# Splitting the layer-normalised activations in fp16 where they lie and transposing them by DMA instead of on TensorE

## The reference, cut to what matters

```python
h = relu(hypergraph_conv(layernorm(x), adj, W1, b1))      # [512, 512] for each graph
h = layer_norm(h, gamma, beta)                            # over the 512 hidden features
y = hypergraph_conv(h, adj, W2, b2)                       # begins with h @ W2.T: [512,512] @ [512,256]
x = x + y + ...                                           # then the router, four experts and an RMS norm
```

## Time and profile before

| | us |
|---|---|
| median of 3 runs (lowest, highest) | 759.8 (759.52, 761.4) |
| the profiled execution's own time | 757.32 |
| its span, first to last instruction | 755.8 |
| TensorE busy | 707.7 (94%) |
| VectorE busy | 655.9 (87%) |
| ScalarE busy | 469.8 (62%) |
| GpSimd busy | 266.9 (35%) |
| TensorE's transposes of hn (L1311, 256 instructions), busy | 36.9 |

### The profile page before, as it was taken

The page is one execution under the profiler, slowest core; times in us unless marked ns, Lnnn a source line. Parts: engine busy times, 40 slices in busy tenths (PEclk is TensorE's granted clock), DMA queues, the critical chain, the costliest instruction groups (busy, mean ns, idle before and its releaser), DMA issues.

```text
span 755.8 us, 16636 instructions
## 1 busy us (share of the span) xinstructions
PE 707.7 (94%) x5645; PEld 490.0 (65%) x5645; DVE 655.9 (87%) x1564; ACT 469.8 (62%) x906; POOL 266.9 (35%) x639
## 2 busy tenths in 40 slices
PE   4787999999999999999999999999999999999983
PEld 3365684857758585775848576684857668485672
DVE  3878988899998889999888999988898998888777
ACT  4555857566585856658584665858476585846653
POOL 4132424142442515244251524425152443504233
PEclk9989999999999999999999999999999999999997
DMA  8437528184572817457282845728284662717112
GB/s 292 163 54 226 112 77 230 30 240 96 180 153 74 231 31 242 88 185 148 77 228 32 243 86 188 145 82 224 36 249 77 200 133 89 189 28 196 29 29 56
DMA packets 40713, 103.26 MB, mean 137 GB/s; under 512 B 4337, under 2 KB 5489, under 8 KB 40689
## 3 DMA queue, kind: packets, MB, share of 16 engines
q1 hardware_dynamic: 29456, 69.92, 28.2%
q0 software_dynamic: 11232, 33.04, 24.2%
HBM read 69.91 MB, written 16.25 MB: 114 GB/s over the span
## 4 chain that ended last, share of the span: by engine, by line
PE 59%; DVE 24%; issue 6%; ACT 4%; DMA 3%; POOL 1%; SPq 1%; DVEq 1%; POOLq 0%; ACTq 0%
PE bank L1256 15%; PE bank L1258 14%; PE bank L1257 14%; PE bank L1344 4%; PE bank L1343 4%; PE bank L1311 3%; DVE a1l L900 3%; DVE ybn L976 3%; DVE x L970 2%; DVE yf L959 2%; DVE h L724 2%; DVE xtl L1028 2%; DVE xbn L733 2%; DMA x2o<-ob 2%; PE bank L1304 2%
## 5 line engine op out<-in xcount | busy, mean ns | idle before, releaser
L493 ACT ACTIVATE silu<-bank,ebcol,ksc 128x512 f32<-128x512 f32 x120 | 92.5, 771 | 38.6 <-PE bank L1258 38.3
L1256 PE MATMUL bank<-xth,ewh 128*128 128x512 f16 (+1 forms) x272 | 99.6, 366 | 1.4 <-DVE ewl L764 1.4
L1258 PE MATMUL bank<-xth,ewl 128*128 128x512 f16 (+1 forms) x272 | 99.7, 366 | 0.0
L1257 PE MATMUL bank<-xtl,ewh 128*128 128x512 f16 (+1 forms) x272 | 99.7, 366 | 0.0
L371 POOL TENSOR_TENSOR yme<-yms,epsrms 128x4 f32<-128x4 f32 (+1 forms) x17 | 3.4, 200 | 238.8 <-ACT ysq L528 230.9
L1256 PE MATMUL bank<-w2h,hnth 128*128 128x256 f16 x256 | 70.4, 275 | 0.0
L1257 PE MATMUL bank<-w2l,hnth 128*128 128x256 f16 x256 | 70.4, 275 | 0.0
L1258 PE MATMUL bank<-w2h,hntl 128*128 128x256 f16 x256 | 70.4, 275 | 0.0
L511 ACT ACTIVATE hnth<-bank 128x512 f16<-128x512 f32 x64 | 38.0, 594 | 38.1 <-PE bank L1311 38.1
L534 ACT ACTIVATE a1h<-bank,be 128x256 f16<-128x256 f32 x64 | 26.8, 470 | 54.8 <-PE bank L1395 51.5
L637 ACT ACTIVATE uh<-bank,be 128x256 f16<-128x256 f32 x64 | 26.8, 470 | 53.3 <-PE bank L1344 53.3
(11 more groups left out here) (253 smaller groups left out, 2086.9 us busy)
## 6 DMA issues: line engine op xcount, KB each, us to landing
adjin<-adj SPq DMA_DIRECT2D x16, 1024.0 KB, 5.4
adjtin<-adjt SPq DMA_DIRECT2D x16, 1024.0 KB, 6.3
xin<-x SPq DMA_DIRECT2D x16, 512.0 KB, 4.2
xb<-xn SPq DMA_DIRECT2D x16, 512.0 KB, 8.4
xb<-x POOLq DMA_DIRECT2D x16, 512.0 KB, 8.7
xb<-b POOLq DMA_DIRECT2D x16, 512.0 KB, 5.4
out<-x SPq DMA_DIRECT2D x15, 512.0 KB, 6.9
x2o<-ob SPq DMA_DIRECT2D x15, 512.0 KB, 10.4
```

What stands on the lines that cost most here:

```text
L493: af(silu[:, i % 4, :], bank[E_BANK[i]][:, :], ACT.Silu, bias=ebcol[:, i:i + 1], scale=ksc[:, 2:3]).then_inc(silu_dn, 1)
L1256: mm(outp, lh, rh, start=first, stop=False)
L1257: mm(outp, lh, rl, start=False, stop=False)
L1258: return mm(outp, ll, rh, start=False, stop=last)
```

## The change

ScalarE writes the high part of hn, as it lies, into the first half of a tile's row of a new buffer hnp (`hn_high`, 128 x 512 fp16), and VectorE the low part into the second half (`hn_low`). When both halves of tile t are there, SyncE issues one DMA transpose, SBUF to SBUF, of 128 x 1024 fp16 (256 KB) into hnt, whose eight blocks of 128 x 128 are the four of the high part and the four of the low part. `v_tile(g, t)` waits for this DMA. TensorE's 16 transposes in each graph, their PSUM banks and the reads of these banks are gone. The two splits of each tile are now right behind its norm. SyncE's list is written out for all graphs instead of looped.

```diff
-        hnth, hntl = sb("hnth", [P, CT, KH * P], F16), sb("hntl", [P, CT, KH * P], F16)
+        hnp, hnt = sb("hnp", [P, CT, 2 * DH], F16), sb("hnt", [P, CT, 2 * KH, P], F16)
...
@@ SyncE, at the end of body
+                if conv:
+                    for t in range(CT):
+                        sp.wait_ge(hnp_lo, 4 * g + t + 1)
+                        sp.dma_start_transpose(hnt[:, t, :, :], hnp[:, t, :]).then_inc(hnt_in[t], 16)
...
-            steps(sp, body, tail)
+            steps(sp, body, tail, unrolled=True)
...
@@ ScalarE
-            def hnt_part(act, g, t):
-                act.wait_ge(hnt_rdy, 4 * g + t + 1)
-                af(hnth[:, t, :], bank[HNT_BANK[t]][:, :], ACT.Copy, scale=HS).then_inc(hnt_hi, 1)
+            def hn_high(act, g, t):
+                act.wait_ge(hn_dn, 4 * g + t + 1)
+                act.wait_ge(hnt_in[t], 16 * g)
+                af(hnp[:, t, 0:DH], hn[:, t, :], ACT.Copy, scale=HS).then_inc(hnp_hi, 1)
...
@@ VectorE
-            def hnt_part(g, t):
-                dve.wait_ge(hnt_hi, 4 * g + t + 1)
-                STT(hntl[:, t, :], bank[HNT_BANK[t]][:, :], HS, hnth[:, t, :], ALU.mult, ALU.subtract).then_inc(hnt_lo, 1)
+            def hn_low(g, t):
+                dve.wait_ge(hnp_hi, 4 * g + t + 1)
+                STT(hnp[:, t, DH:2 * DH], hn[:, t, :], HS, hnp[:, t, 0:DH], ALU.mult, ALU.subtract).then_inc(hnp_lo, 1)
...
@@ TensorE
-            def transposed_h(g, t):
-                pe.wait_ge(hn_dn, 4 * g + t + 1)
-                if t >= 2:
-                    pe.wait_ge(hnt_lo, 4 * g + t - 1)
-                for k in range(KH):
-                    ins = nc.tensor.transpose(bank[HNT_BANK[t]][:, P * k:P * k + P], hn[:, t, P * k:P * k + P], ident[:, :])
-                ins.then_inc(hnt_rdy, 1)
...
             def v_tile(g, t):
-                pe.wait_ge(hnt_lo, 4 * g + t + 1)
+                pe.wait_ge(hnt_in[t], 16 * g + 16)
...
-                    ins = three(b, hnth[:, t, P * k:P * k + P], hntl[:, t, P * k:P * k + P], w2h[:, k, :], w2l[:, k, :],
+                    ins = three(b, hnt[:, t, k, :], hnt[:, t, KH + k, :], w2h[:, k, :], w2l[:, k, :],
```

More of the change, by code:

```diff
@@ L66, in build @@
         DEG = slice(64, 64 + CT)
-        A3_BANK, HNT_BANK, V_BANK, U_BANK, B3_BANK = (0, 3, 4, 1), (2, 0, 2, 0), (1, 2), (3, 4), (1, 2)
+        A3_BANK, V_BANK, U_BANK, B3_BANK = (0, 3, 4, 1), (1, 2), (3, 4), (1, 2)
         XT_BANK, R_BANK, E_BANK, O_BANK = (5, 6), 7, (5, 6, 7, 5, 6, 7, 5, 6), (6, 7)
@@ L181, in build @@
         x_in, adj_in, adjt_in, x1_st, out_st = sem("x_in"), sem("adj_in"), sem("adjt_in"), sem("x1_st"), sem("out_st")
-        deg_rdy, a3_rdy, hnt_rdy = sem("deg_rdy"), sem("a3_rdy"), sem("hnt_rdy")
+        deg_rdy, a3_rdy = sem("deg_rdy"), sem("a3_rdy")
         a1_rdy, a2_rdy, v_rdy, u_rdy, b3_rdy = (sem(n) for n in ("a1_rdy", "a2_rdy", "v_rdy", "u_rdy", "b3_rdy"))
@@ L188, in build @@
         e_rdy = sem("e_rdy")
-        a1_hi, relu_dn, hn_dn, hnt_hi, u_hi, x2_dn, sq_dn, xn_dn = (
-            sem(n) for n in ("a1_hi", "relu_dn", "hn_dn", "hnt_hi", "u_hi", "x2_dn", "sq_dn", "xn_dn"))
+        a1_hi, relu_dn, hn_dn, hnp_hi, u_hi, x2_dn, sq_dn, xn_dn = (
+            sem(n) for n in ("a1_hi", "relu_dn", "hn_dn", "hnp_hi", "u_hi", "x2_dn", "sq_dn", "xn_dn"))
         a2_hi, v_hi, xt_hi, ct_hi = (sem(n) for n in ("a2_hi", "v_hi", "xt_hi", "ct_hi"))
@@ L199, in build @@
         r_step = sem("r_step")
-        a1_lo, z_dn, hbn_dn, hstat, hnt_lo, u_lo, x1_dn, ybn_dn, xbn_dn, yf_dn = (
-            sem(n) for n in ("a1_lo", "z_dn", "hbn_dn", "hstat", "hnt_lo", "u_lo", "x1_dn", "ybn_dn", "xbn_dn", "yf_dn"))
+        a1_lo, z_dn, hbn_dn, hstat, hnp_lo, u_lo, x1_dn, ybn_dn, xbn_dn, yf_dn = (
+            sem(n) for n in ("a1_lo", "z_dn", "hbn_dn", "hstat", "hnp_lo", "u_lo", "x1_dn", "ybn_dn", "xbn_dn", "yf_dn"))
         ystat, be_max, be_dn = sem("ystat"), sem("be_max"), sem("be_dn")
+        hnt_in = [sem(f"hnt_in{t}") for t in range(CT)]
         a2_lo, v_lo, xt_lo, ct_lo, y_dn = (sem(n) for n in ("a2_lo", "v_lo", "xt_lo", "ct_lo", "y_dn"))
@@ L219, in build, with steps @@
         T_E, T_XT, T_R, T_MB, T_O, T_ROW = (1, 2, 5), (5, 0), (3, 4), ((6, 7), (0, 3)), (6, 7, 4, 5), CG * P
-        def steps(eng, body, tail):
+        def steps(eng, body, tail, unrolled=False):
             body(eng, 0, conv=True, ffn=False, late=False, prep=True)
@@ L225, in steps @@
             body(eng, 2, conv=True, ffn=True, late=True, prep=True)
-            with eng.Fori(3, N - 1) as g:
-                body(eng, g, conv=True, ffn=True, late=True, prep=True)
+            if unrolled:
+                for g in range(3, N - 1):
+                    body(eng, g, conv=True, ffn=True, late=True, prep=True)
+            else:
+                with eng.Fori(3, N - 1) as g:
+                    body(eng, g, conv=True, ffn=True, late=True, prep=True)
             body(eng, N - 1, conv=True, ffn=True, late=True, prep=False)
@@ L600, in body @@
                 if conv:
+                    hn_high(act, g, 0)
                     norm_h(act, g, 1)
@@ L604, in body @@
                 if conv:
-                    if not ffn:
-                        hnt_part(act, g, 0)
+                    hn_high(act, g, 1)
                     norm_h(act, g, 2)
@@ L612, in body @@
                 if conv:
[L613 to L616, removed]
+                    hn_high(act, g, 2)
                     norm_h(act, g, 3)
-                if conv:
-                    if ffn:
-                        hnt_part(act, g, 1)
                 if ffn:
                     expert(act, f, 6)
+                if conv:
+                    hn_high(act, g, 3)
+                if ffn:
                     expert(act, f, 7)
                 if conv:
-                    hnt_part(act, g, 2)
-                    hnt_part(act, g, 3)
                     v_part(act, g, 0)
@@ L1082, in body @@
                     h_aggr(g, 3)
+                    hn_low(g, 0)
                     if not ffn:
-                        hnt_part(g, 0)
                         setup_mag_ew()
@@ L1087, in body @@
                     combine(f, 1)
+                if conv:
+                    hn_low(g, 1)
+                if ffn:
                     combine_sum(f, 1)
-                if conv and ffn:
-                    hnt_part(g, 0)
+                if conv:
+                    hn_low(g, 2)
+                    if not ffn:
+                        setup_mag_c()
                 if ffn:
@@ L1093, in body @@
                 if conv:
-                    hnt_part(g, 1)
-                    if not ffn:
-                        setup_mag_c()
+                    hn_low(g, 3)
                 if ffn:
@@ L1099, in body @@
                     combine(f, 3)
-                if conv:
-                    hnt_part(g, 2)
-                if ffn:
                     combine_sum(f, 3)
                 if conv:
-                    hnt_part(g, 3)
                     if not ffn:
@@ L1387, in body @@
                     for e in range(CT):
-                        if ffn and e == 0:
-                            pe.wait_ge(hnt_lo, 4 * g)
                         if ffn and e == CG:
@@ L1465, in body @@
                     mask_rows(f, 2, g, conv)
-                if conv:
-                    transposed_h(g, 0)
-                    transposed_h(g, 1)
                 if ffn:
@@ L1477, in body @@
                     v_tile(g, 0)
-                    transposed_h(g, 2)
                     v_tile(g, 1)
-                    transposed_h(g, 3)
                     v_tile(g, 2)
```

## The result

The changed kernel takes 826.4 us (median of 4 runs, 822.5 to 829.1) where the kernel before takes 759.7 beside it: a ratio of 1.087, 95% interval 1.082 to 1.092. Forecast were 827, with 0.71 for slower. The loss has the forecast size, but it does not lie in the places that the working named.

What follows compares the result with a forecast made beforehand. TensorE, 94% busy, was taken as the bound, VectorE nearly second. Per step +3.3 us landing and +0.9 clock, times 16, gave 67 us on 757.3: 824, or 827 as median; likeliest case 765 to 900, whole range 752 to 1000.

Steps and rivals of the forecast that it cites:

- the clock: TensorE's granted clock may fall behind the waits for transposes; 2.6 us a step if so, a third taken: +0.9.
- the fourth landing: Fourth transpose of a step lands at 363.0, so `v_tile` 3 starts then instead of at 359.72: +3.3 us a step.
- TensorE's transposes go: Removing TensorE's transposes frees 1.75 us a step, 28 us in all, the most that the change could give.
- the experts on VectorE are not earlier: VectorE's first ctl comes no sooner, so the output product gains at most 0.3 us, taking nearly all of the 1.75.
- the fast case: Rival: DMA transposes take under 1.6 us of queue each, so not slower, 756 to 757 us; chance 0.29.
- The splits move, and cost the same: ScalarE's high and VectorE's low parts keep count and cost; low parts end at 350.3, 352.1, 354.0 and 355.9.
- The DMA transpose, D = 2.4 us: Each tile's DMA takes 2.4 us of the queue (D), between 0.8 and 7.4, plus 2.0 fixed from issue to landing.
- Sharing: GpSimd's xb<-b, issued inside the four transposes, delays them by 0 to 5.4 us; 1.1 taken.
- If D is below 1.6 us the step is not longer: Bar for fast transposes: 350.3 + 2.0 + 4D + 1.1 then stays below 359.72, the present start of `v_tile` 3.
- Four waits of about 1 us a step: On TensorE, bias matmuls of `v_tile` wait for the DMA of hnt, 1 to 2 us each, four times a step.
- SyncE's order: Transposes holding SyncE could make xin or adjin late; needs more than 13 us, so priced only within the slow case.
- Step 0 counted like the others: Step 0 has no experts to put between, but was given the same loss as every other step.

Runs made afterwards that it cites:

- run 1: The changed kernel, with GpSimd's accumulating DMA xb<-b issued only when the step's fourth transpose has landed: 764.5 us, ratio 1.009 to the kernel before.
- run 4: The changed kernel plus sixteen useless matmuls on TensorE ahead of the wait of `v_tile` 1: 802.3 us, ratio 1.059 to the kernel before.
- run 2: The changed kernel without its four DMA transposes; `v_tile` reads hnp as it lies, so transposition is left out: 759.1 us, ratio 1.000 to the kernel before.
- run 11: DMA version with late xb<-b and reordered engine lists (761.1 us), but graph 0 transposed by TensorE: 756.5 us, ratio 0.998 to the kernel before.
- run 3: The changed kernel with the four DMAs copying the same 256 KB per tile without transposing: 785.5 us, ratio 1.037 to the kernel before.

## Why the prediction was right, point by point

**The direction and the size came out; the wait and the clock were right, what makes the DMA late was wrong, and the size is luck.** TensorE waits for the DMA and the clock falls behind the wait: runs 1 and 4 show both. The sum had +3.3 us a step for the fourth landing and +0.9 for the clock, 67 us in all; measured were 67. But of the 3.3 only 1.1 were for xb<-b, so by the sum 2.2 would stay without it, and run 1 shows nothing in the steady steps. Nor is the ordinary step 4.2 us longer: its fourth transpose landed 35.0 us behind adjin (at 307.88), not 37.1 (363.0 less 325.88), and it is 3.4 us longer, the hole of 3.45 plus 1.7 of the clock less the freed 1.75. The mean of 4.2 comes about only with the slow steps, 6 to 7 us longer, which I had not foreseen. Terms too large and too small cancelled.

**"TensorE's transposes go", at most 28 us, and "the experts on VectorE are not earlier": right.** Run 2 shows it by itself. The forecast for the fast case was a gain of at most 0.3 us a step; it came out as 0. The 1.73 us in front of the first output product are the 1.75 us of the earlier trace rows over again.

**"The splits move, and cost the same": right.** The low parts were forecast 1.8 to 1.9 us apart; in the step above they start at 331.78, 333.67, 335.57 and 337.47. The first ends 24.6 us behind adjin, where my times for it (350.3, adjin at 325.88) give 24.4.

**The DMA transpose, D = 2.4 us: wrong.** It is 1.4, and the landing in the clear is 3.0 to 3.1 us instead of 4.4, so that the fixed part is 1.6 and not 2.0. As the four are issued 1.9 us apart, in the clear none stands behind another, and the sum of four D has no place there. I had taken the middle, in ratio, between the price by bytes and the price by packets; but a packet of 256 bytes takes 0.021 us, a third of what the packets of the first 10 us took the earlier trace rows, which were 1.3 KB long. The 261 GB/s that the Trainium skill gives ("DMA: Bandwidth & Descriptors", section "Latency and other measured facts"), 1.0 us for a tile, comes nearer: 1.4 us is 187 GB/s. The trace does not agree with the estimate of 10.5 us from the Trainium skill's 1309 ns for one block ("VectorE: DVE Perf Modes", section "The three transpose paths"); eight blocks in one DMA took 1.4 us.

**"Sharing", 1.1 us: wrong, and it was the main term.** I gave xb<-b one microsecond, between not giving way at all and giving way wholly. The transposes give way wholly, as the queues' rows from 335.0 to 338.5 show. It puts 3.2 us on the second in an ordinary step and 5.8 in a slow one. The row for it was there: xb<-xn takes 8.4 us beside other DMAs for the size that xb<-b moves in 5.4. Run 1 shows that this alone, with its effect on the clock, is worth 62 us.

**"If D is below 1.6 us the step is not longer": wrong as stated.** D was below 1.6 and the step was longer. The bar took the sharing of 1.1 for granted. With the contention removed (run 1) the fast rival's step came out as worked out, the same as before. Its 3.3 us from split to landing does not follow from its own 2.0 + 0.8; it happens to lie near the 3.1 measured.

**Four waits of about 1 us a step: wrong.** It is one, of 3.2 to 6.3 us, ahead of `v_tile` 1, as only the second transpose is late enough to show. Nor do later tiles take longer to land: 3.0, 6.3, 5.3 and 3.1 us. That is also the likely reason why **the clock** cost more than the third of 2.6 us that I took: the hole is as long as those of step 0. Run 4 gives 1.5 us a step in place of 0.9.

**SyncE's order: right to be priced at nothing.** adjin and xin were covered. **Step 0 counted like the others: about right** (4.8 us for a mean of 4.2), but its cause is different: there are no experts to hide the landing, and it is lost with the late xb<-b too (run 1) and gone when TensorE transposes graph 0 (run 11).

## What to carry to other kernels

Before a transfer is put on the path, list what the other queues issue in the same few microseconds, above all accumulating DMAs, and give those that aren't urgent a wait: here one line was worth 62 us of 67. Work taken from the busiest engine gave nothing by itself here (run 2), where another engine's result comes 0.3 us before it is needed; look at how late each input of the next instruction is, not at shares of busy time. And when a product is moved, find its reader, and what stands behind the reader in its engine's list.

## What the runs showed that I had not expected

- A 256-byte packet of a transpose takes 0.021 us of a DMA engine; a transpose of 256 KB takes 1.4 us of the queue and holds SyncE 1.23 us while it is issued (a plain copy of the same size: 0.47 us). When the queue is behind, the issue itself stalls, up to 4.2 us (5.0 in run 4), and the DMA after it is issued later.
- 0.6 us decide: a transpose issued just with the accumulating DMA lands in 8.8 to 9.1 us, one issued 0.6 us or more behind it in 6.0 to 6.8. The later one waits until xb<-b is through, the earlier one runs mixed with it and both are slow. Why was not tried; a plain copy issued at the same moment lands in 2.4 (run 3).
- Of the 15 holes of 3.2 to 6.3 us ahead of `v_tile` 1 in steps 1 to 15, twelve are followed by a lower clock and three are not. In the step above, with a hole of 3.45 us, the clock was at half for 3.4 us, which cost 1.7: there a wait costs half as much again as it lasts. Useless matmuls in the hole gained 24 us.
